# Two-layer transformer on one core: where VectorE does the query rotations and two MLP operations of the first layer

## What is computed

```python
h = (x - mu) * rsqrt(var + eps) * (1 + scale) + shift
q = rope(h @ Wq.T); c = h @ Wkd.T; k = rope(c @ Wku.T); v = c @ Wvu.T
x = x + (softmax(mask(q @ k.T / sqrt(32))) @ v) @ Wo.T
```

```python
h = ada_rms(x); q = rope(h @ Wq.T); k = rope(h @ Wk.T); v = h @ Wv.T
x = x + (softmax(q @ k.T / 8) @ v) @ Wo.T
h = ada_rms(x)
x = x + (silu(h @ Wg.T) * (h @ Wu.T)) @ Wd.T      # 2048 wide
```

## Time and profile before

| | us |
|---|---|
| median of 3 runs | 1804.07 |
| lowest and highest run | 1800.82, 1804.49 |
| span of the profiled execution | 1804.9 |
| PE busy in it | 1717.2 (95%) |
| VectorE busy | 1152.3 (64%) |
| ScalarE busy | 945.9 (52%) |
| GpSimd busy | 398.8 (22%) |

### The profile page before, as it was taken

How to read it: one execution, slowest core, us unless ns; L and a number is a source line. 1 busy time by engine, 2 the same in 40 slices (tenths; PEclk the granted TensorE clock), 3 DMA queues, 4 the chain that set the end, 5 groups by cost and what they waited for, 6 DMA issues and landing times.

```text
span 1804.9 us, 37773 instructions
## 1 busy us (share of the span) xinstructions
PE 1717.2 (95%) x12440; PEld 931.9 (52%) x12440; DVE 1152.3 (64%) x2858; ACT 945.9 (52%) x2769; POOL 398.8 (22%) x556
## 2 busy tenths in 40 slices
PE   6686899999999999999999999999999999999999
PEld 2344445555455545555455554555455554555444
DVE  6759566675667657685576756676576855767320
ACT  3836456364664538564483646645385644835320
POOL 3438587011111112111110111111121111101120
PEclk9676999999999999999999999999999999999999
DMA  7866489462784449662593637944485725936220
GB/s 245 152 181 115 126 197 253 98 117 82 163 175 94 80 119 184 133 118 78 127 194 91 119 88 161 171 95 82 115 192 125 123 73 138 196 85 112 100 70 24
DMA packets 527231, 234.30 MB, mean 130 GB/s; under 512 B 476336, under 2 KB 493744, under 8 KB 527024
## 3 DMA queue, kind: packets, MB, share of 16 engines
q1 hardware_dynamic: 511472, 175.09, 48.9%
q10 hardware_dynamic: 15552, 56.63, 10.1%
HBM read 90.09 MB, written 16.78 MB: 59 GB/s over the span
## 4 chain that ended last, share of the span: by engine, by line
PE 77%; DVE 10%; DMA 6%; issue 4%; ACT 2%; SPq 1%; DVEq 0%; POOL 0%; ACTq 0%
PE up L1427 8%; PE up L1429 8%; PE up L1428 8%; PE gate L1427 7%; PE gate L1429 7%; PE gate L1428 7%; PE y L1427 4%; PE y L1428 4%; PE y L1429 4%; PE bank L1427 4%; PE bank L1429 4%; PE bank L1428 4%; DMA prob_t<-prob 3%; PE bank L1454 2%; DVE prob L1113 2%
## 5 line engine op out<-in xcount | busy, mean ns | idle before, releaser
L864 ACT ACTIVATE bank<-bank,low 128x128 f32<-128x128 f32 (+2 forms) x768 | 302.7, 395 | 68.2 <-DVE low L1106 35.0
L702 POOL TENSOR_TENSOR inner_t<-inner,inner_t 128x512 f16<-128x512 f32 x128 | 149.0, 1164 | 662.7 <-ACT inner_t L1045 662.6
L1113 DVE TENSOR_TENSOR prob<-bank,prob 128x512 f16<-128x512 f32 (+1 forms) x320 | 202.8, 634 | 54.3 <-ACT prob L873 53.4
L873 ACT ACTIVATE prob<-bank 128x512 f16<-128x512 f32 (+1 forms) x320 | 178.7, 558 | 73.3 <-DMA prob_t<-prob 44.5
L1427 PE MATMUL up<-mlp,ring 128*128 128x512 f16 x512 | 194.9, 381 | 12.8 <-DVE inner L1392 12.8
L1382 DVE SCALAR_TENSOR_TENSOR silu<-silu,gate 128x512 f32<-128x512 f32 x128 | 87.9, 687 | 183.8 <-ACT silu L1039 183.0
L1427 PE MATMUL gate<-mlp,ring 128*128 128x512 f16 x512 | 194.0, 379 | 1.4 <-DVE mlp L1078 0.9
L1429 PE MATMUL up<-mlp,ring 128*128 128x512 f16 x512 | 194.9, 381 | 0.0
L1428 PE MATMUL up<-mlp,ring 128*128 128x512 f16 x512 | 194.9, 381 | 0.0
L1429 PE MATMUL gate<-mlp,ring 128*128 128x512 f16 x512 | 194.0, 379 | 0.0
L1428 PE MATMUL gate<-mlp,ring 128*128 128x512 f16 x512 | 193.9, 379 | 0.0
(11 more groups left out here) (182 smaller groups left out, 4041.8 us busy)
## 6 DMA issues: line engine op xcount, KB each, us to landing
ring<-wgu_dram ACTq DMA_DIRECT2D x108, 512.0 KB, 3.8
x_in<-x_dram SPq DMA_DIRECT2D x18, 512.0 KB, 3.8
x_res<-x_mid SPq DMA_DIRECT2D x16, 512.0 KB, 3.0
wgu_dram<-ring SPq DMA_DIRECT2D x16, 512.0 KB, 3.6
out_dram<-x_res SPq DMA_DIRECT2D x32, 256.0 KB, 2.3
prob_t<-prob SPq DMA_TRANSPOSE x256, 3.5
inner_t<-wd_t_dram SPq DMA_DIRECT2D x4, 1024.0 KB, 8.7
ring<-wg_t_dram SPq DMA_DIRECT2D x16, 256.0 KB, 4.1
```

The costliest lines, as they stand in the source:

```text
L702: pool.tensor_tensor(inner_t[:, 1, f, :], inner[:], inner_t[:, 0, f, :], ALU.subtract).then_inc(inner_low, 1)
L864: ins = act.activation(bank_[:, at:at + wid], bank_[:, at:at + wid], ACT.Exp, bias=low[:, j % BANKS, k:k + 1], scale=-1.0, accum_out=total)
L873: act.activation(terms(prob[:, g % SLOTS, 0, :], layer, j), terms(work_bank[USE[f"unit{layer}", j] % BANKS][:], layer, j), ACT.Copy).then_ ...
L1113: dve.tensor_tensor(terms(prob[:, slot, 1, :], layer, j), terms(work_bank[USE[name] % BANKS][:], layer, j), terms(prob[:, slot, 0, :], lay ...
```

## The change

Only VectorE's order changes, in `layer0`, and only for pairs with an MLP in between (1 to 7). The rotation of tile 0, sequence 0 moves ahead of the MLP operations of the steps "keys.0" and "keys.1" (inner 2 and gate 3); the rotation of sequence 1 stays behind them, but moves ahead of those of "query1.0" (inner 3). For tile 1, a new function does inner 5 ahead of the two low halves. No instruction is added or removed.

```diff
+            def early_inners(m, step):
+                if m is None:
+                    return 0
+                parts = parts_at(m, step)
+                for k, part in enumerate(parts):
+                    f, done = part // 4, part % 4 + 1
+                    if f >= FCH or done == 2:
+                        return k
+                    if done == 4:
+                        inners(m, [f])
+                return len(parts)
+
-            def between(m, *steps):
-                for step in steps:
+            def between(m, *steps, skip=0):
+                for k, step in enumerate(steps):
                     if m is not None:
-                        for part in parts_at(m, step):
+                        for part in parts_at(m, step)[0 if k else skip:]:
...
-                between(m, "keys.0", "keys.1", "query1.0", "query1.1")
                 for t in range(TILES):
                     for s in BOTH:
                         need(dve, y_full, count(n, 8, 2 * t + s + 1))
                         need(dve, stack_low, count(n, 12, 2 * t + s + 1))
                         rotate0(ybank[s][:], 0, t, H0, *rotated(s, D), rope_terms)
+                        if t == 0 and s == 0:
+                            between(m, "keys.0", "keys.1")
+                    if t == 0:
+                        between(m, "query1.0", "query1.1")
                     rope_adds(n, 1 + t, D)
+                    early = early_inners(m, f"stack{t}.0") if t == 1 else 0
                     for s in BOTH:
...
-                    between(m, f"stack{t}.0", f"stack{t}.1")
+                    between(m, f"stack{t}.0", f"stack{t}.1", skip=early)
```

## The result

| | before | changed |
|---|---|---|
| median of 4 runs, us | 1803.12 | 1794.15 |
| lowest and highest run | 1800.82, 1804.49 | 1790.25, 1795.71 |
| span of the profiled execution | 1804.9 | 1788.3 |

The ratio is 0.994, with an interval of 0.9928 to 0.9952: 10.8 us faster, between 8.7 and 13.0. The prediction's 1790.5 was 3.7 us too low. Its wide range, 1785.5 to 1797.8, holds the result, the narrower one of the forecast alone, 1787.5 to 1794, just misses it, and the direction is right.

What follows compares the result with a forecast made beforehand. PE, busy 95% of the span, was taken to bound the kernel, so its waits on VectorE counted: 10.6 us from pairs 2 to 7 plus 3.0 from pair 1, 13.6 off 1804.07, gives 1790.5; range 1785.5 to 1797.8.

Steps and rivals of the forecast that it cites:

- the forecast alone: The main case without its rivals: 1790.5 us, own range 1787.5 to 1794, chance 0.62.
- The first wait: PE's wait for VectorE's rotation before tile 1's query product, pairs 2 to 7: goes whole, 0.85 us a pair.
- Inner 3's thin cover: The rotation of sequence 1 ends at 870.29, 0.14 us before inner 3, which waits for PE until 870.43 anyway.
- The adds beside POOL: Tile 0's adds, moved earlier, lie where POOL works on chunk 3: cost taken as zero, 1.9 us would be covered.
- The second wait: PE's wait for inner 5 before chunk 6's up product, pairs 2 to 7: shrinks from 1.61 to 0.14 us lost.
- the new one: New PE wait for gate 6 before chunk 7's gate product: 0.55 us, holding the gain to 1.77 us a pair.
- The six pairs together: Pairs 2 to 7, each gaining 1.77 us: 10.6 us.
- Pair 1: Its 3.69 us wait for inner 5 shrinks to under 1 us; 3.0 us gained, between 1.2 and 4.75.
- Gate 6's end at 251.9: In pair 1, gate 6 waits for low halves and ACT to about 251.9, so at most 4.75 us is won.
- The price of a fall of the clock: In pair 1, at 1.2 GHz twelve up matmuls take 5.09 us instead of 2.6; avoiding it gives back 2.5 us.
- A lead eaten by the attention: Rival: the probabilities' chain bounds PE later in the pair, leaving 6.3 us, 1797.8; chance 0.16.
- The rule from the Trainium skill: A two-SBUF-input VectorE operation and a GpSimd operation reading SBUF share a lock; one add blocks for one POOL instruction at most.

Runs made afterwards that it cites:

- the third measurement: The unedited change timed a third time, beside the kernel with both the tanh and the chunk 9 load reordered; 1793.32 us, ratio 0.9952 to the kernel before.

## Why the prediction was right, and where it was off

- **The first wait.** 0.85 us in each of pairs 2 to 7 by the prediction; the kernel with the rotations alone shows a floor lower by 0.85 and 4.7 us in all, where 5.1 were worked out. Right in mechanism and size. Inner 3's thin cover held: it started 9.11 us behind the first mark, 9.10 before.
- **The adds beside POOL.** Taken at zero. In pairs 3 to 7 they took 1.28, as before; instead the low halves behind them took 2.07 and not 1.29, and VectorE then stood idle for 4.34 us ahead of gate 4. The slack was there as forecast; the operation that met POOL was the next one.
- **The second wait and the new one.** Forecast: 0.14 and 0.55 lost, 1.77 gained. The rows give 0.14 and 0.56, and the floor fell by 1.76. What was named as late next, ACT's copies ahead of the tanh, was shown by taking them out of the way: 0.57 came back.
- **The six pairs together.** 10.6 us; with the change in these pairs alone 12.1 us (9.7 to 14.6) were measured, so this term alone can account for the whole 10.8.
- **Pair 1.** This term was the least certain, and probably too large. Forecast 3.0, between 1.2 and 4.75. Alone it measured 2.3 (0.5 to 4.0), and the three traces of the change have a pair 1 that is 3.57, 2.33 and 0.95 us shorter than in the one trace of before. What was forecast for the place itself came true: PE waits 0.55 us for inner 5 where it waited 3.69, the granted clock is 1.00 from 246 to 254, and the gate product of chunk 7 comes 5.0 us earlier, counted from the first mark of the pair. The step that was off comes behind it. The prediction let a part of the lead be given back to POOL, but looked for it at 301.15, by 0.30 us. The earlier PE ran into the split of chunk 9 and waited 2.2 us in every one of seven traces; in four of them the clock fell behind it, which cost 1.7 us more in the trace that was lined up. SP's queue was named as one that doesn't move, but got no number: the load stood at 255.36, behind two transposes. Gate 6's end at 251.9 and its gain of 1.2 us stand on no row that was shown.
- **The price of a fall of the clock.** The prediction has 2.5 us, from one execution. With inner 5 late in pair 1 the wait is 3.7 us in two more traces; with the rotations alone the first five matmuls behind it still start 0.22 apart and the twelve take 4.07 us instead of 5.09, with pairs 2 to 7 alone 4.24. So the price depends on the execution: the up product lost 1.5 to 2.5 us in these three.
- **The sum.** 13.6 us against 10.8: the forecast gain lies above the whole interval, 8.7 to 13.0. With the term of pair 1 at its measured 2.3 the sum would be 12.9, just inside the interval; the parts measured alone add up to more than the whole, so where the other 2.1 us go, if they are there at all, is not shown. The first ten executions of the change fall in two groups some 5 us apart, 1789.1 to 1790.3 and 1793.7 to 1795.7. The ten of the third measurement don't: they spread from 1789.7 to 1802.0. A fall of the clock in pair 1 with what follows it (2.6 us) and a pair that waits for probabilities (one of 1.4 to 1.6 us above the floor in each of two traces of the change) are two parts of the spread; which execution gets how many was not found.
- **The profiled execution of before** was not a middling one: it holds a pair 1.5 us above the floor. The prediction puts it 0.8 above the median, but compares a span with a time: in the changed kernel's execution the time, 1790.25, is 2.0 above the span, 1788.3, which by estimate makes 1806.9 of the span of 1804.9, 2.8 above the median. Summing against it did no harm, since I carried over the difference and not the span, but the span's fall of 16.6 us overstates the gain.
- **The rivals.** A lead eaten by the attention was real for inner 5 alone: 0.9981, where the six intervals add up to 0.5 us less than six times 114.22 and not to the 5.5 that were worked out. In the full change it takes little. The rule from the Trainium skill ("SBUF — State Buffer", "Who interferes with whom"), weighed against the change, had the right pair of engines: where the two meet, both records are longer, 1.47 us instead of 1.16 on POOL and 2.07 instead of 1.29 for the low halves. It cost nothing, as the slack said.

## What to carry to other kernels

When a wait of the busiest engine goes, price the next operation that it needs, by which engine and by what ahead of it; here this gave the fall of the floor to 0.01 us. In a start-up stretch that looks like a steady one, follow the earlier engine on to the next resource with its own queue, a load for instance, and give that a time too. A local gain is not yet a gain of the whole: inner 5 alone took 0.90 off PE's path at its place, kept it to the end of one pair in six, and brought 3.4 us (1.3 to 5.6) where 9 were worked out. Whether the halves bring less apart than together, 3.4 and 4.7 against 10.8, these intervals don't tell. And the time of a whole kernel, good to some 2 us here, can't rank orders that differ by less; the same stretch taken in each pair of a trace can.

## What the runs showed that I had not expected

- PE's clock fell behind a wait of 2.2 us in some executions and not in others of the same kernel: of the three traces of the changed kernel, one granted 0.67 from 266 to 270, the two others 1.00 behind their wait. PE had been busy for 1.8 of the 4 us ahead in each, so what decides it is not shown.
- Pairs of most kernels here repeat to 0.03 us when nothing waits for a transpose, and differ by up to 1.9 us when something does. What makes a transpose late in one pair and not in the next was not found.
